# Six groups of source rows gathered from x without pacing, and GpSimd's wait for queries from group 12 on, in a two-layer graph network kernel

## The chip, the cores and the metric

The kernel runs on one core of one Trainium2 chip. The metric is the device time of one execution in microseconds. For the kernel before it is 2708.49 us, the median of three runs that lie between 2705.53 and 2711.26 us. The profile beside it is of one execution, whose span from the first to the last recorded instruction is 2246.1 us.

## The reference, cut to what matters

There are 3125 nodes with 128 features each and 103125 edges sorted by destination. The first layer is graph attention with four heads, followed by a small dense network; the second is a radial message passing layer over the same edges.

```python
# layer 1
q, k, v = x @ Wq.T + bq, x @ Wk.T + bk, x @ Wv.T + bv          # (3125, 4, 32)
alpha = sum(q[dst] * k[src], -1) / sqrt(32)
e = exp(alpha - segment_max(alpha, dst)[dst])
a = e / segment_sum(e, dst)[dst]
conv = segment_sum(a[:, :, None] * v[src], dst) + x @ Wskip.T + bskip
# ... Wout, layer norm, 128-512-128 MLP, layer norm; x = layernorm(x + that)
# layer 2
Y1 = sqrt(3) * edge_vec / (norm(edge_vec) + 1e-12)              # edge vectors
w = mlp(radial_embedding(edge_length)).reshape(-1, 4, 32)
messages = f(w, (x @ W_up)[src], Y1)                            # 256 numbers per edge
x = layernorm(x + segment_sum(messages, dst) @ W_out / 16)
```

## The kernel before, in words

Edges are handled in tiles of 128 and groups of four tiles (512 edges); there are 202 groups (`NQ`), and real edges fill 806 tiles (`REAL`). The kernel has four stages.

**Start.** SyncE loads the source numbers `src_col`, the weights `wqkv` and `bqkv` and the transposed x in four quarters (`xT`). ScalarE issues six loads of its own at once: `dst_rows`, `first_rows`, `consts`, `dst_i`, `base_i`, `r_col`. TensorE computes the queries of 26 node tiles (seven fours of tiles) and then keys and values of 25 (thirteen pairs); VectorE adds the bias (`q_sb` and `kv_sb` count its steps), SyncE writes the query table `q_tab` to DRAM, and ScalarE writes the key and value table `kv_tab`.

**Layer 1 over the edges.** For every group, GpSimd gathers four times 128 rows by source number, with one indirect DMA per tile. From group `XQ` on it gathers key and value rows from `kv_tab` (256 numbers per row) into a ring of 16 slots. For the first `XQ` groups the table isn't written yet, so it gathers rows of x itself (128 numbers) from an input in DRAM, and TensorE turns them (`x_turned`), ScalarE copies them (`x_copied`), TensorE multiplies them with the weights (`x_keys`), and VectorE adds the bias and puts the result into the slot (`x_biased`). The gathers of x have pacing waits: tiles 2, 4 and 6 wait for `q_sb`, tiles from 8 on for `kv_sb`. After them GpSimd waits for all of `kv_tab` and `q_tab`. The loop over groups on every engine is a list of slots. In slot q, TensorE makes the queries of group q+1 (`queries`, which counts `qe_ready`) from a window of `q_tab`; VectorE multiplies queries and keys (`product`), reduces them (`scores`), weighs values of the group 12 slots back (`weigh`, which counts `msg_ready`) and adds summed tiles to the accumulator (`add_tile`). Every eight groups a chain of small steps over four slots does the softmax of that batch. TensorE sums messages in `sums` (`sum_ready`). SyncE's queue loads, per group, `rel` (`numbers`) and four query windows (`windows`), ahead by up to six groups, and in between the rest: at group 3 the edge vectors `attr_col` and the writing of `r_far`, at group 5 a wait for `r_far`, from group 6 on the pieces of the radial embedding, at group 18 a wait for the finished edge directions (`yprep`) and the load of `x_rows`.

GpSimd's own waits in this stage are: from group 16 on for the ring slot (`msg_ready`), from group 6 on for the queries two groups back (`qe_ready` at q - 1), and before the third tile of a group for sums 15 groups back (`sum_ready`).

VectorE has, besides, one-time work on 128x808 arrays: the difference `rel_rows` ahead of the first query bias, the squares of edge vectors (`square_norms`) in slot 5 and the directions in slots 7 and 8 (`directions`).

**Dense part,** then **layer 2 over the edges**, again with one indirect DMA per tile, from `up_tab`, and then the output.

Of the kernel before, what the change touches and what calls it, by code (L numbers as in the profile page):

```python
# [14 lines left out]
P = 128  # L15
# [3 lines left out]
U32 = mybir.dt.uint32  # L19
ALU = mybir.AluOpType  # L20
# [16 lines left out]
RING = 16  # L37
# [4 lines left out]
CHAIN = 4  # L42
XQ = 4
LAG = BQ + CHAIN
# [10 lines left out]
REAL = -(-E // P)  # L55
HS = BT + 1
BIG = 1e38
assert NQ % 2 == 0 and H * BT == P and NT * P >= E and 4 * NT <= NW
# [85 lines left out]
def build(nc, a, out):  # L144
    with ExitStack() as ctx:
# [209 lines left out]
        def _(sp):  # L355
# [6 lines left out]

            sp.wait_ge(rel_ready, 1)
            sp.dma_start(rel_far.rearrange("(p n) -> p n", p=P), rel_rows).then_inc(rel_out, 16)
            for g, tiles in enumerate(fours):
                sp.wait_ge(q_sb, g + 1)
                sp.dma_start(q_tab[tiles[0] * P:(tiles[-1] + 1) * P, :].rearrange("(t p) f -> p t f", p=P),
                             q_stage[:, g, 0:len(tiles) * D].rearrange("p (t f) -> p t f", f=D)).then_inc(q_out, 16)
# [44 lines left out]
            for q in range(NQ):  # L413
# [6 lines left out]
                if q == 3:  # L420
                    batch_rows(0)
                    sp.dma_start(yvec[:], a["attr_col"]).then_inc(ld["attr"], 16)
                    sp.dma_start(b2f[0:1, 0, :], a["mlp_b2"]).then_inc(b2_in, 16)
                    sp.wait_ge(r_ready, 2)
                    sp.dma_start(r_far.rearrange("(p n) -> p n", p=P), r_col).then_inc(r_out, 16)
                if q == 5:
                    sp.wait_ge(r_out, 16)
                if emb_step(q, 6) is not None:
                    spread_lengths(emb_step(q, 6))
# [48 lines left out]
        def _(pool):  # L478
            pool.wait_ge(ld["src"], 16)
            for q in range(XQ):  # L480
                for k in range(QT):
                    t = q * QT + k
                    if k % 2 == 0 and 1 <= t // 2 <= 3:
                        pool.wait_ge(q_sb, t)
                    if k % 2 == 0 and t // 2 >= 4:
                        pool.wait_ge(kv_sb, 3 * (t // 2) - 11)
                    nc.gpsimd.indirect_dma_start(
                        xg[:, q, k, :], None, a["x_tab"],
                        bass.IndirectOffsetOnAxis(src_col[:, t:t + 1].bitcast(U32), 0)).then_inc(rows_in[q], 16)
            pool.wait_ge(kv_out, 16 * len(pairs))  # L490
            pool.wait_ge(q_out, 16 * len(fours))
            for q in range(XQ, NQ):
                if q >= RING:
                    pool.wait_ge(msg_ready, q - RING + 1)
                if q >= 6:
                    pool.wait_ge(qe_ready, q - 1)
                for k in real_tiles(q):
                    t = q * QT + k
                    summed = len([j for j in range(NQ) if weigh_slot(j) <= q - 3])
                    if k == 2 and summed:  # L500
                        pool.wait_ge(sum_ready, summed)
                    nc.gpsimd.indirect_dma_start(  # L502
                        kvr[:, q % RING, k, :], None, kv_tab,
                        bass.IndirectOffsetOnAxis(src_col[:, t:t + 1].bitcast(U32), 0)).then_inc(rows_in[q % RING], 16)

# [5 lines left out]
            for q in range(NQ):  # L511
# [4 lines left out]
                for k in real_tiles(q):  # L516
                    t = q * QT + k
                    if k == 2 and q >= 6:
                        pool.wait_ge(sum2_ready, QT * (q - 2))
                    nc.gpsimd.indirect_dma_start(  # L520
                        upr[:, q % RING, k, :], None, up_tab,
                        bass.IndirectOffsetOnAxis(src_col[:, t:t + 1].bitcast(U32), 0)).then_inc(rows_in[q % RING], 16)

# [271 lines left out]
        @block.scalar  # L795
        def _(act):
            act.dma_start(dst_rows, a["dst_rows"]).then_inc(ld["rows"], 16)
            act.dma_start(first_rows, a["first_rows"]).then_inc(ld["rows"], 16)
# [82 lines left out]
            for q in range(-3, LAST_SLOT):  # L881
# [11 lines left out]
                if q in SKIPS:  # L893
                    skipped(SKIPS.index(q))
                if q == 6:
                    act.wait_ge(yprep, 5)
# [118 lines left out]
        def _(dve):  # L1015
# [11 lines left out]
            v.memset(tile_sum[0:1].rearrange("p k (h t) -> p k h t", h=H)[:, :, :, 0], 0.0).then_inc(rows_ready, 1)  # L1027
            dve.wait_ge(ld["rows"], 32)
            v.tensor_tensor(rel_rows, dst_rows, first_rows, ALU.subtract).then_inc(rel_ready, 1)

            dve.wait_ge(ld["w"], 32)
            for g, tiles in enumerate(fours):
# [3 lines left out]
                                ps[:, 4 + g % 4, 0:n * D].rearrange("p (t f) -> p t f", t=n),  # L1036
                                bqkv[:, 0:D].unsqueeze(1).to_broadcast([P, n, D]), ALU.add).then_inc(q_sb, 1)
            for g, tiles in enumerate(pairs):
                n = len(tiles)
# [5 lines left out]
            def x_biased(g):  # L1045
                dve.wait_ge(xkv_mm, g + 1)
                for i in range(2):
                    v.tensor_tensor(kvr[:, g, 2 * i:2 * i + 2, :], ps[:, x_banks(g)[i], :].rearrange("p (t f) -> p t f", t=2),
# [187 lines left out]
            for q in range(LAST_SLOT):  # L1236
# [31 lines left out]
                if q == 4:  # L1268
                    bias_pieces()
                if q == 5:  # L1270
                    square_norms()
                if q in (7, 8):
                    directions(q - 7)
                if q == 34:
# [7 lines left out]
                if q == 11:  # L1282
                    dve.wait_ge(yprep, 12)
                    dve.wait_ge(r_out, 16)
                    dve.wait_ge(acc_zero, 1)


# [312 lines left out]
```

## Time and profile before

| | |
|---|---|
| runs, us | 2705.53 to 2711.26, median 2708.49 |
| profiled execution: span, us | 2246.1 (what lies around the span isn't recorded) |
| indirect DMAs of GpSimd | 16 from x, 790 from kv_tab, 806 from up_tab |
| GpSimd busy on the 790 from kv_tab, us | 762.0, first at 40.4, last at 1049.6 |
| GpSimd busy on the 806 from up_tab, us | 768.4, first at 1198.4 |
| PE, DVE, ACT, POOL busy, share of the span | 77%, 77%, 56%, 69% |

The trace gives each instruction its start and length, and the idle time of its engine before it with what ended it. "PE" is TensorE, "DVE" VectorE, "ACT" ScalarE, "POOL" GpSimd, "SPq" and "ACTq" the DMA issues of SyncE and ScalarE. GpSimd issues an indirect DMA for 0.94 to 0.95 us and takes 0.30 us before the next one; those 0.30 us are counted as idle, put down to "issue" or to a semaphore that was set before.

### The profile page before, as it was taken

What the parts mean: (1) busy time and instruction counts of PE and PEld (TensorE: products, weight loads), DVE (VectorE), ACT (ScalarE), POOL (GpSimd) and SP (SyncE); (2) the same over time, 40 slices, a digit from 0 to 9 for tenths busy, and PEclk for the clock granted to TensorE, in tenths of its full rate; (3) what the DMA queues carried; (4) which work ended last, traced back from release to release, by engine and by line L of the source; (5) the groups of instructions that cost most, each with busy time, mean ns of one, the idle gap of its engine ahead of it and who ended that gap; (6) DMA issues with size and microseconds to landing.
All of it is one profiled execution on the core that took longest, in us unless ns stands there. A gap on an engine that the chain in (4) does not pass through costs nothing. (4 is left out here: it accounts for less than half of the span.)

```text
span 2246.1 us, 37849 instructions
## 1 busy us (share of the span) xinstructions
PE 1725.3 (77%) x9754; PEld 1318.5 (59%) x9754; DVE 1727.8 (77%) x4978; ACT 1261.2 (56%) x3062; POOL 1552.3 (69%) x1617
## 2 busy tenths in 40 slices
PE   5657667676777767666588888888898889888886
PEld 5456556565666656555465565655565556556555
DVE  4778787776777777778686888888888888888887
ACT  1567667576675775766365455444444444545444
POOL 4777777777777777775015777777777777777773
PEclk9676776766666676776598999999999999999998
DMA  9787767677666676774001222222222222222221
GB/s 292 197 250 200 197 182 197 185 195 198 185 193 191 190 201 184 192 201 113 1 21 47 57 57 57 56 56 57 56 57 56 56 57 56 57 57 57 57 55 51
DMA packets 242692, 270.81 MB, mean 121 GB/s; under 512 B 46237, under 2 KB 201971, under 8 KB 241965
## 3 DMA queue, kind: packets, MB, share of 16 engines
q0 software_dynamic: 64224, 157.52, 25.8%
q1 hardware_dynamic: 173980, 105.40, 16.6%
q10 hardware_dynamic: 4272, 5.48, 0.7%
q8 instruction: 80, 1.31, 0.2%
q14 instruction: 136, 1.11, 0.2%
HBM read 256.06 MB, written 12.15 MB: 119 GB/s over the span
## 5 line engine op out<-in xcount | busy, mean ns | idle before, releaser
L520 POOL DMA_INDIRECT rows<-up_tab,src_col x806 | 768.4, 953 | 264.9 <-issue 239.9
L502 POOL DMA_INDIRECT rows<-kv_tab,src_col x790 | 762.0, 965 | 253.1 <-issue 218.2
L763 PE MATMUL ps<-hotT,rows 128*128 128x128 f32 x3232 | 426.0, 287 | 128.0 <-DVE rows L1452 128.0
L763 PEld LDWEIGHTS ps<-hotT,rows 128*128 128x128 f32 x3232 | 390.5, 197 | 201.7 <-DVE rows L1452 200.5
L1421 DVE TENSOR_TENSOR acc<-acc,ps 128x256 f32 x808 | 339.1, 420 | 95.6 <-DVE acc L1421 40.3
L582 PE MATMUL ps<-hots,msg 128*128 128x128 f32 x1616 | 337.8, 375 | 78.4 <-DVE msg L1135 72.1
L582 PEld LDWEIGHTS ps<-hots,msg 128*128 128x128 f32 x1616 | 295.0, 274 | 116.2 <-DVE msg L1135 110.3
L1116 DVE TENSOR_TENSOR work<-ps,rows 128x512 f32<-128x512 f32 x202 | 138.9, 688 | 205.5 <-issue 122.7
L571 PE MATMUL ps<-qwin,hotT 128*128 128x128 f32 x1088 | 217.5, 365 | 78.8 <-DVE work L1116 70.1
L816 ACT ACTIVATE hotT<-consts,nrel 128x128 f32<-128x128 f32 x808 | 255.5, 389 | 4.7 <-PE ps L763 4.7
L1152 DVE TENSOR_TENSOR acc<-acc,ps 128x128 f32 x808 | 227.4, 281 | 39.3 <-DVE acc L1152 4.2
L816 ACT ACTIVATE hots<-consts,nrel 128x128 f32<-128x128 f32 x808 | 255.5, 386 | 3.4 <-PE ps L582 3.2
L571 PEld LDWEIGHTS ps<-qwin,hotT 128*128 128x128 f32 x1088 | 197.5, 271 | 94.3 <-issue 75.2
L752 PE MATMUL ps<-weights,rows 128*128 128x256 f32 x808 | 231.2, 409 | 0.0
L978 ACT ACTIVATE rows<-ps,vecs 128x512 f32<-128x512 f32 x101 | 69.4, 687 | 265.9 <-PE ps L735 265.9
L984 ACT ACTIVATE rows<-ps,vecs 128x512 f32<-128x512 f32 x101 | 69.4, 687 | 237.4 <-PE ps L741 237.4
L752 PEld LDWEIGHTS ps<-weights,rows 128*128 128x128 f32 x808 | 138.5, 191 | 99.5 <-issue 88.7
L1436 DVE TENSOR_TENSOR rows<-rows,yvec 128x384 f32<-128x384 f32 x202 | 116.1, 575 | 96.8 <-DMA rows<-up_tab,src_col 95.8
L834 ACT ACTIVATE hotT<-rel,consts 128x512 f32<-128x512 bf16 x202 | 143.3, 709 | 7.0 <-DMA rel<-rel_far 5.5
L571 PE MATMUL ps<-exb,hotT 128*128 128x128 f32 x528 | 109.3, 375 | 43.6 <-DVE work L1116 37.7
L861 ACT COPY tile_max<-ps 1x256 f32<-1x256 f32 x26 | 9.4, 361 | 237.0 <-PE ps L611 237.0
L1126 DVE TENSOR_REDUCE alpha<-work 128x16 f32<-128x512 f32 x202 | 137.5, 681 | 0.8 <-issue 0.5
(178 smaller groups left out, 2496.6 us busy)
## 6 DMA issues: line engine op xcount, KB each, us to landing
qwin<-q_tab SPq DMA_DIRECT2D x544, 64.0 KB
rel<-rel_far SPq DMA_DIRECT2D x202, 128.0 KB
exb<-q_tab SPq DMA_DIRECT2D x264, 64.0 KB
rows<-up_tab,src_col POOLq DMA_INDIRECT x806
rows<-kv_tab,src_col POOLq DMA_INDIRECT x790
rows<-emb_rows SPq DMA_DIRECT2D x202, 16.0 KB
weights<-r_far SPq DMA_DIRECT2D x25, 128.0 KB, 3.7
emb_rows<-weights SPq DMA_DIRECT2D x25, 128.0 KB, 3.5
```

What stands on the lines that cost most here:

```text
L502: nc.gpsimd.indirect_dma_start(kvr[:, q % RING, k, :], None, kv_tab, bass.IndirectOffsetOnAxis(src_col[:, t:t + 1].bitcast(U32), 0)).then_ ...
L520: nc.gpsimd.indirect_dma_start(upr[:, q % RING, k, :], None, up_tab, bass.IndirectOffsetOnAxis(src_col[:, t:t + 1].bitcast(U32), 0)).then_ ...
L571: mm = pe.matmul(ps[:, 1 + q % 2, k * P:(k + 1) * P], hotT[:, q % TURNS, k, :], qrows(q)[:, k, :], start=True, stop=True)
L582: mm = pe.matmul(ps[:, 4 + j % SUMS, k * P:(k + 1) * P], msg0[:, j % 3, k, :], hot_of[:, j % HOTS, k, :], start=True, stop=True)
L752: mm = pe.matmul(to[:, k], h2s[:, u, (2 * half + k) * P:(2 * half + k + 1) * P], wt(W_M2, 2 * P).rearrange("p (s f) -> p s f", s=2), start ...
L763: mm = pe.matmul(ps[:, 4 + 2 * (q % 2) + k // 2, (2 * (k % 2) + m) * P:(2 * (k % 2) + m + 1) * P], left[:, q % 2, k, :], hot2[:, q % 2, k, ...
L816: op = nc.scalar.activation(to[:, k, :], iota, ACT.Square, bias=nrel[:, q * QT + k:q * QT + k + 1])
L834: nc.scalar.activation(to, rel[:, q % RELS, :], ACT.Square, bias=consts[:, K_NEGP:K_NEGP + 1]).then_inc(squareT_ready, 1)
L1116: v.tensor_tensor(work[:, q % 2, :].rearrange("p (t f) -> p t f", t=QT), ps[:, 1 + q % 2, :].rearrange("p (t f) -> p t f", t=QT), kvr[:, q ...
L1126: v.tensor_reduce(to, work[:, q % 2, :].rearrange("p (t h c) -> p t h c", t=QT, h=H), AX.X, ALU.add).then_inc(score_ready, 1)
L1152: v.tensor_tensor(to, to, ps[:, 4 + j % SUMS, k * P:(k + 1) * P], ALU.add).then_inc(acc_step, 1)
L1421: v.tensor_tensor(to, to, ps[:, 4 + 2 * (q % 2) + k // 2, (k % 2) * 256:(k % 2) * 256 + 256] .rearrange("p (m f) -> p m f", m=2), ALU.add) ...
```

## The change

- `XQ` goes from 4 to 6: six groups (24 indirect DMAs instead of 16) gather rows of x and go through TensorE. The pacing waits of these gathers are taken away. Two groups fewer (8 indirect DMAs) gather from `kv_tab`.
- GpSimd's wait for queries holds from group 12 (`FREE`) on, instead of 6.
- ScalarE's six loads are issued after the second quarter of `xT` has landed.
- `rel_rows` is computed after the fifth query bias instead of ahead of the first, and SyncE writes it after the fifth write to `q_tab`.
- The load of the edge vectors goes from group 3 to group 8, their squares from slot 5 to 11, ScalarE's root from 6 to 12, the directions from slots 7 and 8 to 13 and 14, and VectorE's wait for them from 11 to 16. SyncE's wait for them stays at group 18.
- `x_biased(4)` waits for the writes of `q_tab`, whose staging lies in the same bytes as slots 4 and up.
- The very last tile gathers only its real rows (85 of 128).

```diff
-XQ = 4
+XQ = 6
+FREE = 12
...
-            sp.wait_ge(rel_ready, 1)
-            sp.dma_start(rel_far.rearrange("(p n) -> p n", p=P), rel_rows).then_inc(rel_out, 16)
             for g, tiles in enumerate(fours):
+                if g == 5:
+                    sp.wait_ge(rel_ready, 1)
+                    sp.dma_start(rel_far.rearrange("(p n) -> p n", p=P), rel_rows).then_inc(rel_out, 16)
                 sp.wait_ge(q_sb, g + 1)
...
                 if q == 3:
                     batch_rows(0)
-                    sp.dma_start(yvec[:], a["attr_col"]).then_inc(ld["attr"], 16)
...
+                if q == 8:
+                    sp.dma_start(yvec[:], a["attr_col"]).then_inc(ld["attr"], 16)
...
             for q in range(XQ):
                 for k in range(QT):
                     t = q * QT + k
-                    if k % 2 == 0 and 1 <= t // 2 <= 3:
-                        pool.wait_ge(q_sb, t)
-                    if k % 2 == 0 and t // 2 >= 4:
-                        pool.wait_ge(kv_sb, 3 * (t // 2) - 11)
                     nc.gpsimd.indirect_dma_start(
...
-                if q >= 6:
+                if q >= FREE:
                     pool.wait_ge(qe_ready, q - 1)
...
         def _(act):
+            act.wait_ge(ld_x[1], 16)
             act.dma_start(dst_rows, a["dst_rows"]).then_inc(ld["rows"], 16)
...
-                if q == 6:
+                if q == 12:
                     act.wait_ge(yprep, 5)
                     nc.scalar.activation(ysq0, ysq0, ACT.Sqrt).then_inc(yprep, 1)
...
-            dve.wait_ge(ld["rows"], 32)
-            v.tensor_tensor(rel_rows, dst_rows, first_rows, ALU.subtract).then_inc(rel_ready, 1)
...
+                if g == 4:
+                    dve.wait_ge(ld["rows"], 32)
+                    v.tensor_tensor(rel_rows, dst_rows, first_rows, ALU.subtract).then_inc(rel_ready, 1)
...
             def x_biased(g):
                 dve.wait_ge(xkv_mm, g + 1)
+                if g == 4:
+                    dve.wait_ge(q_out, 16 * len(fours))
...
-                if q == 5:
+                if q == 11:
                     square_norms()
-                if q in (7, 8):
-                    directions(q - 7)
+                if q in (13, 14):
+                    directions(q - 13)
...
                 if q == 11:
-                    dve.wait_ge(yprep, 12)
...
+                if q == 16:
+                    dve.wait_ge(yprep, 12)
```

## Rows read from the trace of the kernel before

**Rows 1.** GpSimd's waits, 200 to 1000 us: line, releaser: us, times, longest us
```profile
POOL rows L502 <- issue: 174.9, 574, 0.3
```

**Rows 2.** GpSimd's waits, 0 to 1060 us
```profile
POOL acc L487 <- DVE rows L1035: 8.8, 1, 8.8
POOL rows L502 <- DMA kv_tab<-rows: 4.9, 1, 4.9
```

**Rows 3.** GpSimd's lines: count, busy us, mean ns, idle before
```profile
L502 POOL DMA_INDIRECT rows<-kv_tab,src_col x790 | 762.0, 965 | 253.1 <-issue 218.2 <-PE ps L571 22.4 <-PE ps L582 6.7
L520 POOL DMA_INDIRECT rows<-up_tab,src_col x806 | 768.4, 953 | 264.9 <-issue 239.9 <-DMA up_tab<-exb 19.5 <-PE ps L752 4.3
```

**Rows 4.** GpSimd in order of time: start, length, tile, idle before
```profile
6.29 1.08 POOL L487 DMA_INDIRECT acc<-in_x_tab,src_col  x1 [5.83 <-DMA src_col<-in_src_col]
40.42 0.95 POOL L502 DMA_INDIRECT rows<-kv_tab,src_col  x1 [4.89 <-DMA kv_tab<-rows]
58.40 0.94 POOL L502 DMA_INDIRECT rows<-kv_tab,src_col  x1 [8.03 <-PE ps L571]
63.41 2.33 POOL L502 DMA_INDIRECT rows<-kv_tab,src_col  x1 [0.30 <-issue]
102.39 0.95 POOL L502 DMA_INDIRECT rows<-kv_tab,src_col  x1 [0.30 <-issue]
```

**Rows 5.** Stages of the start: length; busy (count) of PE, PEld, DVE, ACT, POOL; PEclk, DMA share, GB/s
```profile
5.00:10.00 5.00, 0.00 (x0) 0.00 (x0) 1.00 (x1) 0.00 (x0) 2.57 (x2) 1.00 1.02 315
15.00:20.00 5.00, 5.00 (x36) 5.00 (x37) 2.78 (x5) 0.00 (x0) 1.71 (x2) 1.00 0.72 235
35.00:40.00 5.00, 3.60 (x14) 3.09 (x15) 0.94 (x2) 2.67 (x5) 0.53 (x1) 0.76 1.08 359
```

**Rows 6.** DMA issues: count, KB each, us from issue to landing
```profile
kv_tab<-rows ACTq DMA_DIRECT2D x12, 256.0 KB, 5.9
base_i<-in_dst_first ACTq DMA_DIRECT2D x1, 404.0 KB, 11.5
yvec<-in_attr_col SPq DMA_DIRECT2D x1, 1212.0 KB, 7.6
```

**Rows 7.** Issues of ScalarE and SyncE, and the first matmul, in order of time
```profile
12.68 2.05 PE L536 MATMUL ps<-wqkv,xT 128*128 128x128 f32 x8 [12.68 <-DMA xT<-in_xT]
26.96 1.27 SPq L376 DMA_DIRECT2D rel<-rel_far  x2
54.06 0.33 SPq L376 DMA_DIRECT2D rel<-rel_far  x1
69.92 1.90 SPq L387 DMA_DIRECT2D exb<-q_tab  x4
72.80 1.88 SPq L387 DMA_DIRECT2D exb<-q_tab  x4
109.78 0.42 SPq L434 DMA_DIRECT2D acc<-in_x_rows  x1
```

**Rows 8.** VectorE and TensorE from 67 to 103 us, in order of time
```profile
67.24 1.00 DVE L1070 TENSOR_TENSOR acc<-acc 128x808 f32<-128x808 f32 x1
79.81 0.68 DVE L1116 TENSOR_TENSOR work<-ps,rows 128x512 f32<-128x512 f32 x1
84.60 2.68 DVE L1080 RECIPROCAL acc<-acc 128x404 f32<-128x404 f32 x1
87.31 1.42 DVE L1082 SCALAR_TENSOR_TENSOR yvec<-yvec,acc 128x1212 f32<-128x1212 f32 x1
95.27 0.62 DVE L1116 TENSOR_TENSOR work<-ps,rows 128x512 f32<-128x512 f32 x1
99.06 1.92 PE L571 MATMUL ps<-qwin,hotT 128*128 128x128 f32 x8
```

**Rows 9.** VectorE's waits, 200 to 1000 us
```profile
DVE work L1116 <- issue: 111.8, 66, 3.4
DVE work L1116 <- DMA rows<-kv_tab,src_col: 39.0, 25, 2.5
```

More of the change, by code:

```diff
@@ L56 @@
 HS = BT + 1
+LAST_ROWS = E - (REAL - 1) * P
 BIG = 1e38
@@ L501, in _ @@
                         pool.wait_ge(sum_ready, summed)
+                    n = P if t < REAL - 1 else LAST_ROWS
                     nc.gpsimd.indirect_dma_start(
-                        kvr[:, q % RING, k, :], None, kv_tab,
-                        bass.IndirectOffsetOnAxis(src_col[:, t:t + 1].bitcast(U32), 0)).then_inc(rows_in[q % RING], 16)
+                        kvr[0:n, q % RING, k, :], None, kv_tab,
+                        bass.IndirectOffsetOnAxis(src_col[0:n, t:t + 1].bitcast(U32), 0)).then_inc(rows_in[q % RING], 16)
             pool.wait_ge(conv, NCH)
@@ L519, in _ @@
                         pool.wait_ge(sum2_ready, QT * (q - 2))
+                    n = P if t < REAL - 1 else LAST_ROWS
                     nc.gpsimd.indirect_dma_start(
-                        upr[:, q % RING, k, :], None, up_tab,
-                        bass.IndirectOffsetOnAxis(src_col[:, t:t + 1].bitcast(U32), 0)).then_inc(rows_in[q % RING], 16)
+                        upr[0:n, q % RING, k, :], None, up_tab,
+                        bass.IndirectOffsetOnAxis(src_col[0:n, t:t + 1].bitcast(U32), 0)).then_inc(rows_in[q % RING], 16)
         @block.tensor
```

## The prediction

> **What bounds the kernel now.** I read GpSimd's waits first, because its two lines of indirect DMAs fill two long stages. Between 200 and 1000 us it waits 174.9 us for "issue", 574 times, never over 0.3 [rows 1]. So 0.30 us is the gap between two gathers, and a gather costs 0.95 + 0.30 = 1.25 us, a group of four 5.0 us. 790 gathers (762.0 us busy, 253.1 idle before them) are the whole length of layer 1's edge stage [rows 3]. Over the whole start and stage there are only three real stalls: 8.8 us in the gathers of x (a pacing wait) and 4.9 us for `kv_tab` [rows 2], and 8.0 us for queries [rows 4]. In order of time: first gather of x at 6.29, the first from `kv_tab` at 40.42 after 4.89 idle, eight of them (groups 4 and 5), then 8.03 idle until the queries of group 4 are there, and group 6 at 58.40 [rows 4]. Up to the gather at 102.39, the first of group 14, it is 32 gathers in 44.0 us: 1.25 each, and 4 us for some that took longer beside VectorE, such as the one of 2.33 us at 63.41 [rows 4]. VectorE, on the other hand, waits at its product for 111.8 us ("issue") and 39.0 us (rows from `kv_tab`) in the same 800 us [rows 9]: in 20 batches of eight groups that is 7.5 us of slack in each 40 us. Layer 2 has the same form: 806 gathers, 768.4 us busy [rows 3]; the change touches it only in its last tile. So the kernel's end is the time of GpSimd's first gather for group 6, plus 782 gathers (tiles 24 to 805) at 1.25 us, plus a tail and a layer 2 that don't change. What counts is how early group 6 starts and how often GpSimd waits after it.
>
> **Part 1: groups 4 and 5 from x.** Eight gathers leave the `kv_tab` stream: 8 x 1.25 = 10.0 us from the path. They are added to the gathers of x: 24 x 1.25 = 30.0 us. From 6.29 us (perhaps one or two earlier, below) they end at 36.3, about 36.8 with the lengthened ones (the first is 1.08). `kv_tab` releases GpSimd at 40.4 [rows 4], so they hide in idle time: the pacing stall of 8.8 us and the 4.9 us for `kv_tab` [rows 2] are that idle time, 13.7 us against 10.0. If `kv_tab` came much earlier, 36.8 would be the floor: a further gain of 3.6 at most.
>
> **Part 2: no wait for queries before group 12.** The 8.03 us stall [rows 4] goes. With part 1 that is 58.40 - 40.42 = 18.0 us, if `kv_tab` stays where it is.
>
> **Part 3: when `kv_tab` is there.** For it: TensorE starts its first matmul at 12.68, when the first quarter of xT has landed [rows 7], while ScalarE's six loads (five of 404 KB, one of 130) take their share of DMA engines that are full (share 1.02, 315 GB/s) [rows 5]. Deferred, they leave 1.2 MB ahead of that quarter, which I estimate at 7 to 8 us; the last bias of keys comes up to 5 us earlier. Against it: the same bytes still have to move before 40 us, and the engines are full to the end (share 1.08, 359 GB/s, from 35 to 40) [rows 5]. The eight more gathers of 64 KB are 0.5 MB; at 0.33 MB per us that is 1.6 us; the one slack stretch (0.72 from 15 to 20 us) [rows 5] gives 1.4 us back. ScalarE's writes of `kv_tab` stand behind its own late loads in its queue. I take 0 for the sum of all that, with +4.6 us (50 GB/s less for the writes of 3.2 MB) and -3.6 (the floor) as ends. The trace shows no execution with the loads deferred, so the ends are kept for the range.
>
> The Trainium skill (DMA: Bandwidth & Descriptors, "Queues, rings and completion order") says that each DMA engine takes turns between the queues that have work, packet by packet. By that rule the unpaced gathers take from xT's loads and from `kv_tab`'s writes in their own turn, whatever was queued first, and it speaks against the removal of the pacing. No row of before separates the queues' shares in that stretch; by the rule the sum would be about 1.6 us smaller, and without it unchanged.
>
> **Part 4: SyncE's loads and the small moves.** `rel_rows` and its write now come later, `base_i` too (11.5 us to landing) [rows 6]. SyncE's first `rel` goes out at 26.96, when `q_tab` has landed [rows 7]. With issue at 10.5 + 11.5 us `base_i` is there at 22, and `rel_far` (issued at about 17, 10 us) at 27: no change, up to 3 us either way, and only queries hang on it. At group 5 SyncE now stands until 54.06 [rows 7] for `r_far`, which is queued behind the 1212 KB of edge vectors (7.6 us to land) [rows 6]; with these at group 8 it comes about 2 to 3 us earlier. Added work on TensorE, ScalarE and VectorE for two more groups of x lies in slots that wait for SyncE's windows: 0. The last tile: 0.
>
> **Part 5: the gates from group 12 on.** Group 6 at 40.4 puts group 12 at 70.4 and 14 at 80.4. At 12 GpSimd needs queries of group 10. Their windows went out at 69.92, those of group 11 at 72.80 [rows 7]; now I put group 10 at about 66, landing at 70 to 71 behind the edge vectors, queries at 72: a wait of 0 to 2. At 14 it needs queries of group 12. Before, they were made from 99.06 to 100.98 [rows 8] and used at 102.39 [rows 4]: 1.4 us of slack. Product 8 comes at about 64 instead of 79.81 (windows of group 8 and its rows are the later of its inputs); from it to product 10 it was 15.5 us [rows 8], of which 4.5 are directions (0.4 + 2.68 + 1.42, as in the rows of 84.60 and 87.31), which are gone from here: 11.0. Then 5.7 more to the end of queries 12: 64 + 11 + 5.7 = 81. A wait of about 1. The squares (five operations of 1.0 to 1.3 us, the last in [rows 8]; 5.8 us) and directions (2 x 4.5) then slow slots 11 to 14, and after that the chain of batch 1 starts: by the same counting sums 3 to 7 come within 2 us of where GpSimd wants them. The 4 us of lengthened gathers come again, later: 0. I take 2.0 us of waits, between 0 and 8 (8 being the old stall paid again).
>
> **Sum.** -10.0 - 8.0 + 0 + 2.0 = -16.0 us on the span: 2246.1 becomes 2230. The runs' median is 2708.49, which is 462 us more than the span; nothing recorded says whether that lies around the span or within. If around, it stays. If it were spread over the 1612 indirect DMAs, it would be 0.29 us on each; 24 gathers of x would then end at about 43.5, and group 6 would gain 58.4 - 43.5 = 15, with fewer waits at the gates. Both give the same answer to 1 us: 2708.5 - 16 = 2692.5 us.
>
> **Rivals.**
> (a) The gates take most of it back. If the windows of groups 9 to 12 land 6 us later (the edge vectors' load stands before them, and 1212 KB are 4 us of all engines), GpSimd waits at 12 and 14 for 8 to 14 us instead of 2. For it: 1.4 us of slack at group 14. Against: SyncE runs at 2.9 us per group there (69.92 to 72.80) [rows 7], against 5 for GpSimd. Gain 4 to 10: 2698 to 2704.
> (b) The start comes out better: `kv_tab` at 37, no waits at the gates, gain 21 to 22: 2687. For it: TensorE 5 us earlier. Against: full DMA engines.
> (c) `kv_tab` comes late, at 48 or more, since ScalarE's queue has 2.15 MB of loads ahead of the writes and three queues share the engines: gain 10 or less, 2698 to 2701. Against: bytes counted above.
> (d) Slower: SyncE stands at group 18 for the directions, which are now finished in slot 14 and not in slot 8. Before, they were done at 88.7 (87.31 + 1.42) [rows 8] and SyncE came to group 18 at 109.78 [rows 7]: 21 us to spare. Now directions end at about 104 (product 10 at 75; 7 to 8 us for slots 10 and 11; squares 5.8; three slots of 2.2, estimated from three VectorE operations of 0.68; directions 9.0), SyncE is there at about 90 and waits, and with it the windows of group 19, which lie behind a load of 1600 KB; from the directions' end to the queries of 19 it's about 9 us. GpSimd needs these for group 21, at 40.4 + 75 + 2 = 117. So it waits for directions that end after 108, and the kernel is slower than before if they end after 108 + 16 = 124. For that slots 8 to 14 would have to take 60 us instead of 40. Time then 2712 or so.
>
> **How the numbers follow.** The forecast (gain 10 to 20) has 0.70, (a) 0.12, (b) 0.06, (c) 0.07, (d) 0.05. A measurement of this kernel tells 0.2%, 5.4 us, from no change. Of (a) and (c) about 0.07 fall under that, the rest is faster: faster 0.87, same 0.08, slower 0.05. The range for 8 in 10 runs from 2687 (gain 21.5, the floor of part 1) to 2701 (gain 7.5, both late ends at once).
>
> **What would show it right or wrong.** In the changed kernel: 24 gathers of x at 1.25 us with no stall; the first gather from `kv_tab`, now group 6, at 40 +- 3 (part 3); none of GpSimd's waits over 0.3 until group 12, about 30 us later; waits there of 2 us in sum (part 5); the last gather from `kv_tab` at 1033 to 1034 instead of 1049.6; all later stages of the same length. A first matmul that isn't earlier than 12.68, a wait of GpSimd in every batch, or a stage 2 of another length would prove the account wrong.

## The result, and the profile after

The changed kernel takes 2732.04 us (median of 4 runs, 2728.52 to 2733.65) against 2709.88 us before (2705.53 to 2718.27) beside it on the same chip. The ratio is 1.0077, 95% interval [1.0061, 1.0093]. The forecast was 16 us faster; it is 22 us slower.

GpSimd's waits of the kernel after, over the whole span and then for 200 to 1000 us (line, releaser: us, times, longest):

```profile
...
POOL rows L503 <- issue: 195.2, 629, 0.9
POOL rows L503 <- remote: 165.9, 72, 3.2
...
POOL rows L503 <- PE ps L584: 98.5, 50, 3.2
POOL rows L503 <- PE ps L573: 69.4, 28, 31.8
```

```profile
POOL rows L503 <- issue: 124.6, 401, 0.9
POOL rows L503 <- remote: 113.8, 49, 3.2
POOL rows L503 <- PE ps L584: 63.1, 33, 3.2
POOL rows L503 <- PE ps L573: 23.2, 17, 1.9
```

The second fence answers to [rows 1], where "issue" at 0.30 us was nearly all there was. ("remote" is a semaphore that another engine set and of which the profile doesn't tell the instruction.) GpSimd's lines, which answer to [rows 3]:

```profile
L522 POOL DMA_INDIRECT rows<-up_tab,src_col x806 | 794.0, 985 | 433.8 <-issue 202.1 <-PE ps L765 158.8 <-PE ps L754 25.6
L503 POOL DMA_INDIRECT rows<-kv_tab,src_col x782 | 745.2, 953 | 553.8 <-issue 195.2 <-remote 165.9 <-PE ps L584 98.5
```

A gather still costs 0.95 us. What has grown is the idle time: 553.8 us in front of 782 gathers, where 790 had 253.1. Layer 2, which the change touches in one gather, has 433.8 instead of 264.9. So a good part of the difference from the profile shown of before can't be the change (e0 below settles how much). The start, in order of time (start, length, instruction, idle before), answers to [rows 4] and [rows 7]:

```profile
4.13 1.12 POOL L487 DMA_INDIRECT acc<-in_x_tab,src_col  x1 [3.67 <-DMA src_col<-in_src_col]
...
8.96 3.28 PE L538 MATMUL ps<-wqkv,xT 128*128 128x128 f32 x15 [8.96 <-DMA xT<-in_xT]
...
17.62 0.69 DVE L1035 TENSOR_TENSOR rows<-ps,bqkv 128x512 f32<-128x512 f32 x1 [2.89 <-remote]
...
27.48 0.69 DVE L1035 TENSOR_TENSOR rows<-ps,bqkv 128x512 f32<-128x512 f32 x1 [9.16 <-remote]
...
37.99 0.69 DVE L1035 TENSOR_TENSOR rows<-ps,bqkv 128x512 f32<-128x512 f32 x1 [9.82 <-remote]
...
41.15 11.70 ACTq L808 DMA_DIRECT2D kv_tab<-rows  x13
...
58.12 0.95 POOL L503 DMA_INDIRECT rows<-kv_tab,src_col  x1 [24.17 <-DMA kv_tab<-rows]
...
72.37 10.55 SPq L390 DMA_DIRECT2D exb<-q_tab  x4
...
119.56 0.94 POOL L503 DMA_INDIRECT rows<-kv_tab,src_col  x1 [31.78 <-PE ps L573]
```

Two stretches stand out: the gathers of x, in which VectorE's biases come 10 us apart, and groups 6 to 11 from 58 to 88 us, whose queries aren't made. Stretches of the same kernel (length; busy (count) of PE, PEld, DVE, ACT, POOL; PEclk, DMA share, GB/s), which answer to [rows 5]:

```profile
15.00:20.00 5.00, 2.58 (x15) 2.22 (x14) 0.69 (x1) 0.00 (x0) 3.78 (x5) 0.87 1.03 344
...
30.00:35.00 5.00, 1.17 (x2) 0.58 (x2) 0.00 (x0) 0.00 (x0) 3.04 (x4) 0.50 0.28 68
35.00:40.00 5.00, 1.17 (x2) 0.29 (x1) 2.01 (x3) 0.00 (x0) 0.00 (x0) 0.50 0.08 22
...
75.00:80.00 5.00, 0.00 (x0) 0.00 (x0) 0.00 (x0) 0.00 (x0) 3.78 (x5) 0.50 0.48 135
```

While GpSimd gathers without a break, the three other engines come nearly to a stand from 25 us on, and the DMA engines are far from full from 30 us on.

### The profile page after: what moved, and what is told of

The parts are those of the page before. It is cut to its first block and busy times, and to the rows that moved or that the text cites. A ratio compares the mean times of both kernels' runs of the same rounds, so it can differ in the third digit from the quotient of the medians.

```text
span 2731.9 us, 37909 instructions
## 1 busy us (share of the span) xinstructions
PE 1835.2 (67%) x9778; PEld 1411.8 (52%) x9778; DVE 1733.1 (63%) x4982; ACT 1252.8 (46%) x3064; POOL 1567.9 (57%) x1617
## 5 line engine op out<-in xcount | busy, mean ns | idle before, releaser
L503 POOL DMA_INDIRECT rows<-kv_tab,src_col x782 | 745.2, 953 | 553.8 <-issue 195.2
L522 POOL DMA_INDIRECT rows<-up_tab,src_col x806 | 794.0, 985 | 433.8 <-issue 202.1
L765 PE MATMUL ps<-hotT,rows 128*128 128x128 f32 x3232 | 509.0, 316 | 187.9 <-DVE rows L1458 109.7
L765 PEld LDWEIGHTS ps<-hotT,rows 128*128 128x128 f32 x3232 | 466.1, 224 | 261.5 <-DVE rows L1458 153.7
L987 ACT ACTIVATE rows<-ps,vecs 128x512 f32<-128x512 f32 x101 | 69.3, 686 | 631.3 <-remote 625.2
L612 PE MATMUL ps<-consts,fw 128*1 128x128 f32 x52 | 19.0, 366 | 347.0 <-DVE bw L1178 207.3
L754 PE MATMUL ps<-weights,rows 128*128 128x256 f32 x808 | 243.9, 427 | 0.0
L743 PE MATMUL ps<-rows,weights 128*128 128x512 f32 x202 | 127.9, 721 | 16.4 <-ACT rows L981 13.3
```

What stands on the lines that cost most here:

```text
L503: nc.gpsimd.indirect_dma_start(kvr[0:n, q % RING, k, :], None, kv_tab, bass.IndirectOffsetOnAxis(src_col[0:n, t:t + 1].bitcast(U32), 0)).t ...
L522: nc.gpsimd.indirect_dma_start(upr[0:n, q % RING, k, :], None, up_tab, bass.IndirectOffsetOnAxis(src_col[0:n, t:t + 1].bitcast(U32), 0)).t ...
L743: pe.matmul(ps[:, 1, :], wt(W_M1), h1s[:, n % 2, :], start=True, stop=True).then_inc(h2_mm, 1)
L754: mm = pe.matmul(to[:, k], h2s[:, u, (2 * half + k) * P:(2 * half + k + 1) * P], wt(W_M2, 2 * P).rearrange("p (s f) -> p s f", s=2), start ...
L765: mm = pe.matmul(ps[:, 4 + 2 * (q % 2) + k // 2, (2 * (k % 2) + m) * P:(2 * (k % 2) + m + 1) * P], left[:, q % 2, k, :], hot2[:, q % 2, k, ...
```

## Experiments

Ratios are to the kernel before timed beside it on the same chip, with 95% intervals. Before itself measured 2682.35 (e0 to e3), 2712.11 (e4 to e6), 2709.91 (e8 to e11), 2676.10 (e12 to e15) and 2710.34 us (e16 to e18; the same chip as e4 to e6), so times are compared within such a group.

### e0 to e3: which part costs

**e0**, the kernel before, unchanged.

> The kernel before, unchanged, profiled beside the others. Theory T (the trace that the prediction used is of a faster execution than the timed ones): its span comes out near its time, some 2705 us and not 2246, and GpSimd, which stood still only three times in the old trace, waits for other engines in both layers; the gap between group 6 of kv_tab's gathers and the span's start may be the old 58 us. Theory S (the changed kernel alone has stalls, made by its start): the span is near 2250 again and GpSimd's gathers stand 1.25 us apart as before, so that the stalls of 450 us seen after the change belong to the change.

Measured: 0.9983 [0.9966, 1.0000]. The profiled run took 2681.4 us for a span of 2679.6, so 1.8 us lie around the span. The 2246.1 us of the profile ahead of the prediction belong to a much faster execution than any timed one. Waits of e0 from 200 to 1000 us, and its lines:

```profile
POOL rows L502 <- issue: 130.5, 407, 2.4
POOL rows L502 <- remote: 84.6, 43, 3.0
POOL rows L502 <- PE ps L582: 54.6, 24, 3.2
POOL rows L502 <- PE ps L571: 46.0, 29, 2.7
```

```profile
L520 POOL DMA_INDIRECT rows<-up_tab,src_col x806 | 789.3, 979 | 422.0 <-issue 205.2 <-PE ps L763 134.3 <-PE ps L752 33.8
L502 POOL DMA_INDIRECT rows<-kv_tab,src_col x790 | 755.5, 956 | 501.5 <-issue 200.5 <-remote 130.0 <-PE ps L571 84.1
```

In the timed condition GpSimd waits 185.2 us of 800 for the other engines (84.6 + 54.6 + 46.0), in pieces of up to 3.2 us, where the old trace has nothing over the 0.3 us gap [rows 1]. The 433.5 us between the two spans: layer 1 from group 6 to the last gather takes 1230.6 us instead of 991.2 (+239.4), layer 2's gathers 1191.2 instead of 1012.4 (+178.8), all the rest +15.3.

**e1**, the change with its pacing waits put back.

```diff
                     t = q * QT + k
+                    if k % 2 == 0 and 1 <= t // 2 <= 3:
+                        pool.wait_ge(q_sb, t)
+                    if k % 2 == 0 and t // 2 >= 4:
+                        pool.wait_ge(kv_sb, min(13, 3 * (t // 2) - 11))
```

> The changed kernel with the pacing waits of the gathers of x put back (six groups; tiles 2, 4, 6 wait for query biases, tiles from 8 on for key biases). Theory A (the 24 unpaced gathers hold back VectorE's query biases, which came at 11, 14, 18, 27 and 38 us, and with them kv_tab, at 58 us): the biases are 0.9 us apart again, kv_tab is there at about 40 us, and the time falls by 18 to 25 us against the changed kernel, to 2707 to 2714. Theory B (ScalarE's deferred loads, or the order of rel_rows, hold VectorE back): no change, 2730.

**e2**, the change with ScalarE's loads issued at once.

```diff
-            act.wait_ge(ld_x[1], 16)
```

> The changed kernel with ScalarE's six loads issued at once, as before. Theory B (the deferred loads hold VectorE at rel_rows, in front of the sixth query bias, and base_i late): kv_tab is there at 45 us or earlier and the time falls by 12 to 20 us, to 2712 to 2720. Theory A (the unpaced gathers are what holds the start): kv_tab stays at 55 to 60 us and the time within 5 us of 2732.

**e3**, the kernel before with nothing but the later gate.

```diff
-                if q >= 6:
+                if q >= 12:
                     pool.wait_ge(qe_ready, q - 1)
```

> The kernel before with one edit: GpSimd's wait for queries holds from group 12 on. By my prediction's step for the stall of 8 us it gains 6 to 8 us (2701 to 2703). If in the timed executions GpSimd isn't the bound, because other engines are slower than in the old trace, it gains nothing (2708 +- 3), or loses some us by gathers that compete with the query windows.

Measured: e1 1.0045 [1.0025, 1.0065], e2 1.0070 [1.0048, 1.0092], e3 1.0070 [1.0044, 1.0096]. Putting the pacing back brings the first write of `kv_tab` from 41.15 to 18.23 us and the first gather from it to 44.89:

```profile
44.89 0.94 POOL L507 DMA_INDIRECT rows<-kv_tab,src_col  x1 [0.30 <-issue]
...
104.27 0.94 POOL L507 DMA_INDIRECT rows<-kv_tab,src_col  x1 [29.70 <-PE ps L577]
```

In e0, on the same chip, group 6 starts at 63.14 and group 12 at 97.9. So in e1 the start of group 6 is 18.2 us earlier, which is what parts 1 and 2 of the prediction promise, and the wait of 29.70 us at group 12 takes it all back: group 12 is 6.4 us later than in e0. Without ScalarE's wait (e2) the first gather from `kv_tab` comes at 59.7, as late as with it (58.1 in the change), and the loss is the change's. And e3, where one number differs from before, is 0.7% slower by itself. e3 in order of time:

```profile
72.50 14.17 SPq L387 DMA_DIRECT2D qwin<-q_tab  x4
...
83.75 0.69 DVE L1116 TENSOR_TENSOR work<-ps,rows 128x512 f32<-128x512 f32 x1 [26.17 <-remote]
83.77 0.95 POOL L502 DMA_INDIRECT rows<-kv_tab,src_col  x1 [0.30 <-issue]
83.81 0.72 ACT L834 ACTIVATE hotT<-rel,consts 128x512 f32<-128x512 bf16 x1 [17.92 <-remote]
...
84.58 1.83 PE L571 MATMUL ps<-exb,hotT 128*128 128x128 f32 x7 [16.83 <-issue]
...
116.84 0.94 POOL L502 DMA_INDIRECT rows<-kv_tab,src_col  x1 [32.13 <-PE ps L571]
```

From 44.99 to 84.71 GpSimd issues 32 gathers, 1.25 us apart. VectorE stands for 26.17 us in them, ScalarE for 17.92, TensorE for 16.83, and four window loads of SyncE take 14.17 us where they took 1.88 [rows 7]. All four move again within 1 us of the last gather's start. Then GpSimd stands for 32.13 us: group 6 starts 8.2 us earlier than in e0 (54.97), as part 2 says, and group 12 18.9 us later (116.84), so the gate at group 12 gives back all that the missing gate at 6 had saved, and more. It isn't one trace alone. In the change, e1, e2, e4 and e18, VectorE stands for 16 to 24 us in the row of gathers ahead of group 12, and moves again 1.6 to 5.8 us after that row's last gather has started.

### e4 to e6: both parts, one after the other

**e4** is the change again, **e5** the change with `FREE = 6`, **e6** the change with `FREE = 6` and the pacing of e1.

> The changed kernel again, on one chip with the next three, so that the parts can be added up (the other chip gave 1.0077 of the kernel before). My theory now (D): a train of back-to-back indirect DMAs on GpSimd makes the semaphore increments of the other engines arrive late, so that what lengthens a train (no pacing in the gathers of x, no wait before group 12) costs time; it expects 1.006 to 1.009 here too, with group 12 of kv_tab's gathers at 115 to 120 us against 98 before. Rival (R): the loss on the other chip lies in that chip's conditions; then this is within 0.3% of before.

> The changed kernel with GpSimd's wait for queries from group 6 on again (one number, 12 to 6); everything else of the change stays, the unpaced gathers of x too. Theory D: the 24 gathers for groups 6 to 11 no longer form one train, so the stall of 30 us before group 12 goes, and 8 to 15 us of the loss with it: 1.001 to 1.004 of before. Rival R2 (it is the start, up to kv_tab's landing at 58 us, that costs everything): unchanged, 1.007.

> As the last one, and with the pacing waits of the gathers of x put back: of the change there remain six groups from x, the deferred loads of ScalarE and of the edge vectors, and rel_rows' new place. Theory D: both long trains are gone, kv_tab is there at about 44 us, and the eight gathers taken off the kv_tab stream gain at last: 0.994 to 0.999 of before. R2 or a theory in which the extra x groups cost other engines more: 1.000 to 1.003.

Start of GpSimd's gathers in us, from the traces:

| | ratio | group 6 | group 12 | group 20 | last from kv_tab |
|---|---|---|---|---|---|
| e4 | 1.0066 [1.0042, 1.0090] | 58.1 | 115.1 | 167.4 | 1328.2 |
| e5 | 1.0042 [1.0027, 1.0056] | 69.9 | 104.7 | 156.8 | 1317.6 |
| e6 | 0.9997 [0.9984, 1.0011] | 60.6 | 95.8 | 148.1 | 1308.7 |

The later gate costs 10.4 us by group 12 and 10.6 by the last gather (e4 against e5), the missing pacing 8.9 and 8.9 (e5 against e6). The loss arises ahead of group 12 and stays as it is. In the times it is 7.8 and 12.8 us (2729.14, 2721.31, 2708.47). With both undone, the change is level with before: what is left of it, six groups from x among it, is worth nothing. In e6 GpSimd is through with its 24 gathers of x and then stands 17.55 us for the queries of group 4:

```profile
12.64 0.95 POOL L491 DMA_INDIRECT acc<-in_x_tab,src_col  x1 [6.17 <-DVE rows L1039]
...
60.63 0.94 POOL L507 DMA_INDIRECT rows<-kv_tab,src_col  x1 [17.55 <-PE ps L577]
```

### e8 to e11: is it the break between gathers?

**e8**, the kernel before with four memsets of 128x32 behind each group of layer 1, each with a wait for the one before. They write bytes that nobody reads.

```diff
+                    for _ in range(4 if k == 3 else 0):
+                        if rests:
+                            pool.wait_ge(rested, rests)
+                        nc.gpsimd.memset(rest[:], 0.0).then_inc(rested, 1)
+                        rests += 1
```

**e9** has one such memset behind every gather. **e10** is e6 with the gate at the queries of the group before (`qe_ready` at q instead of q - 1). **e11** does the same in layer 2 too (`w_mm` at q).

> The kernel before, with four short memsets on GpSimd (128x32 each, with GpSimd's own semaphore between them, an estimated 0.15 to 0.3 us each) after each group of four gathers of layer 1. If GpSimd alone were the bound (the prediction's account), 198 groups times 0.6 to 1.2 us come on top: 1.04 to 1.09 of before. Theory D (trains of back-to-back indirect DMAs delay the others' semaphore increments): GpSimd's waits, now 260 to 290 us in this stage, take up the memsets, the trains get shorter, and the period of a group stays at 6.3 to 6.4 or falls: 0.97 to 1.01.

> The same work, spread: one such memset after each gather, so that no two gathers of layer 1 follow each other at 1.25 us. Theory D, if only unbroken trains at 1.25 us count: a larger gain than with the four together, 0.95 to 0.98. D, if the mean rate of indirect DMAs counts: the same time as with the four together, within 0.3%. GpSimd as the only bound: 1.04 to 1.09.

> The kernel of e6 (six groups from x, paced; wait for queries from group 6) with the wait one group tighter: gathers of group q wait for the queries of group q - 1 instead of q - 2. Theory D: the trains (mean 4.9 gathers, up to 13) get shorter, increments come in time more often, and the period falls below 6.40: 0.97 to 0.995. Rival L (GpSimd's lead is what hides the landing of the rows): VectorE's product waits for rows more often, 1.00 to 1.03.

> As e10, and in layer 2 too: gathers of group q wait for the edge weights (w_mm) of group q - 1 instead of q - 2. Theory D: layer 2, now 5.95 us per group with trains of 7.7 gathers in the mean, gains in the same way; another 0.5 to 2% over e10. Rival L: layer 2 gets longer by the landing of rows, up to 1% slower than e10.

Measured: e8 0.9753 [0.9728, 0.9778], e9 1.0011 [0.9998, 1.0024], e10 1.0012 [0.9990, 1.0034], e11 1.0133 [1.0095, 1.0172]. First e9 and then e8, GpSimd in order of time:

```profile
200.12 0.95 POOL L504 DMA_INDIRECT rows<-kv_tab,src_col  x1 [0.17 <-issue]
201.08 0.14 POOL L510 MEMSET rest<- 128x32 f32 x1
201.38 0.95 POOL L504 DMA_INDIRECT rows<-kv_tab,src_col  x1 [0.17 <-issue]
```

```profile
205.83 0.95 POOL L504 DMA_INDIRECT rows<-kv_tab,src_col  x1 [0.30 <-issue]
206.78 0.68 POOL L510 MEMSET rest<- 128x32 f32 x4
208.04 0.95 POOL L504 DMA_INDIRECT rows<-kv_tab,src_col  x1 [0.58 <-issue]
```

Both kernels run four memsets per group. In e9 each hides in the 0.30 us between two gathers, which stay 1.26 us apart, so GpSimd's pace is as before and nothing changes. In e8 they make one break of 1.26 us (0.84 in most groups below 16), and the kernel is 2.5% faster although GpSimd has more to do: 101.4 us of memsets. e8 from 200 to 1000 us, and its line:

```profile
POOL rows L504 <- issue: 193.5, 508, 0.9
POOL rows L504 <- remote: 7.4, 11, 1.2
POOL rows L504 <- DVE msg L1142: 4.0, 6, 1.2
POOL rows L504 <- PE ps L589: 2.2, 2, 1.3
```

```profile
L504 POOL DMA_INDIRECT rows<-kv_tab,src_col x790 | 758.9, 961 | 317.2 <-issue 285.1 <-remote 12.4 <-DMA kv_tab<-rows 6.7
```

The waits for other engines are 13.6 us, and a group takes 6.08 us (from 200 us to the end of the stage). In e9, on the same chip, they are 183.5 us and 6.42; in e0, on another, 185.2 and 6.30. A break also slows GpSimd: with it a group can't take less than 6.0 us (three times 1.25, 0.95 and 1.26), without it 5.0. Pauses of the same sum spread evenly over the gathers weren't tried, so whether the break as such helps or the slower pace isn't shown. What the other engines do while GpSimd gathers, counted from the traces of layer 1 by the place of a gather in its row of gathers without a break of over 0.4 us:

```
instructions per us of PE, PEld, DVE and ACT, while the gather at this place runs
place            1-4     5-8     9-12
e0              12.5     8.3     0.5
after           13.2     8.2     0.4
e8              10.1      -       -
e10             11.4     6.5     9.5
```

This counting can't tell cause from effect by itself, since a row also ends where the others have stopped and GpSimd's gate holds it. e10 speaks against taking the length of a row for the whole cause. From 200 us on its rows are 6.9 gathers long in the mean, against 4.9 in e6 (another chip), the period is the same (6.40 and 6.41 us per group), and at places 9 to 12 the others work on; its breaks are fewer and longer, 269.7 us in sum against 280.7. In e11 layer 2 takes 6.12 us per group where e10 takes 5.94 (from 1600 us on), with waits of 205.0 us for "remote" before its gathers: a tighter gate there costs. Of these four expectations of the theory of rows only e8's held: e9 and e10 were to gain and did not, and e11 went with the rival.

### e12 to e15: the change with breaks

**e12** is the change with the four memsets behind each group of x and of layer 1, **e13** the kernel before with them in both layers, **e14** e6 with them in x and both layers, **e15** the kernel before with two per group in layer 1.

> The changed kernel whole, with the four short memsets after each group of gathers of x and of kv_tab (a pause of 1.26 us instead of 0.30, as seen in e8). In e8 the kernel before with the same pauses in layer 1 was 0.9753 of before. Theory D (the change costs time because its trains of 24 gathers hold up the other engines): with trains cut to four the change's cost of 0.7 to 0.8% is gone, and its eight gathers fewer gain: 0.966 to 0.976. Rival E (the change costs by something else, such as the deferred loads or two more groups of x on TensorE and VectorE): the cost stays, 0.981 to 0.985.

> The kernel before with the pause of four memsets after each group of gathers in both layers. Theory D: layer 2, at 5.94 us per group with trains of 7 to 8 gathers, gains too, up to the new floor of 5.95 us of GpSimd's own work per group: since that floor is where it already stands, little, -0.5 to +0.5% over e8, 0.970 to 0.980. If the pauses add to layer 2 instead: 0.98 to 1.01.

> The kernel of e6 (of the change: six groups from x, paced; deferred loads; wait from group 6 on) with the pauses in the gathers of x and in both layers. e6 was 0.9997 of before. Theory D: as e13, less the 8 gathers (10 to 12 us at 1.49 per gather): 0.966 to 0.976. Rival E: as e13 or slower.

> The kernel before with two memsets instead of four after each group of kv_tab's gathers: a pause of some 0.7 to 0.8 us instead of 1.26 (e8) or 0.30 (before). Theory D, if any break of a train over about 0.3 us helps: period 5.5 to 5.7 us, 0.955 to 0.97. If only the mean rate of GpSimd's indirect DMAs counts, half of e8's gain or less: 0.985 to 1.0.

Measured: e12 0.9805 [0.9774, 0.9837], e13 0.9841 [0.9809, 0.9873], e14 0.9865 [0.9832, 0.9897], e15 0.9896 [0.9852, 0.9941]. Two memsets give 1.0% (a group takes 6.18 us; with four, in e13 on the same chip, 6.04), four in layer 1 alone 2.5% on other chips. In layer 2 the breaks lose: 6.03 us per group in e13, 5.89 in e12 (from 1600 us on). e12 and e14 missed the 0.966 to 0.976 that the theory of rows expected of them. e15 missed its 0.955 to 0.97 and lies where it was expected if only GpSimd's mean rate counts (0.985 to 1.0), so the slower pace stays a rival of the break.

### e16 to e18: the change against before, both with breaks, on one chip

**e16** is e8 again, **e17** e12 again, **e18** the change. As in e8 and against the words of its expectation, e16 has no breaks in the gathers of x; e17 has them there too.

> The kernel before with four small memsets on GpSimd (128x32, own semaphore) after each group of x and kv gathers of layer 1. Theory (trains of gathers hold back what the other engines report): about 0.975 of the kernel before again. Rival (the gain was of one chip alone): within 0.5% of before.

> The change with the same rests in the same places. Theory that the change's own loss is made by the longer trains alone: with the trains cut, the change is level with the rested kernel before (within 0.2% of it, on the same chip), or up to 0.6% faster, what the prediction gave it. Rival (the late gate costs by itself, by a wait for the queries of group 12 that no rest takes away): 0.3 to 0.7% slower than the rested kernel before.

> The change as it is, on the same chip as the two rested kernels, so that its loss without rests stands beside its loss or gain with them: 1.006 to 1.009 of before by every theory.

Measured: e16 0.9741 [0.9721, 0.9761] (2634.09 to 2643.35 us), e17 0.9781 [0.9758, 0.9805] (2645.59 to 2659.89), e18 1.0068 [1.0052, 1.0085]. The medians, 2636.46 and 2647.57, are 11.1 us or 0.42% apart, and the two sets of runs don't overlap. So breaks don't cure the change's own loss: they leave 11 of its 18 us, and the rival written down for e17 holds. What they do cure is the start. With the same unpaced gathers of x, `kv_tab`'s first write goes out at 41.09 in e18 and at 21.62 in e17, and the first gather from it starts at 59.03 and 44.17. GpSimd at both ends of the ungated stretch of e17:

```profile
44.17 0.96 POOL L514 DMA_INDIRECT rows<-kv_tab,src_col  x1 [6.00 <-DMA kv_tab<-rows]
...
75.69 0.95 POOL L514 DMA_INDIRECT rows<-kv_tab,src_col  x1 [0.30 <-issue]
76.64 0.69 POOL L490 MEMSET rest<- 128x32 f32 x4
100.15 0.95 POOL L514 DMA_INDIRECT rows<-kv_tab,src_col  x1 [22.82 <-PE ps L585]
```

Stretches of e16 and then of e17, with the columns as above:

```profile
60.00:70.00 10.00, 6.12 (x32) 3.73 (x30) 9.66 (x17) 7.24 (x12) 7.71 (x11) 1.00 0.62 180
70.00:80.00 10.00, 4.73 (x19) 2.97 (x19) 7.95 (x9) 4.20 (x6) 8.01 (x15) 0.82 0.68 191
```

```profile
60.00:70.00 10.00, 5.02 (x15) 4.20 (x16) 1.88 (x3) 1.83 (x3) 7.67 (x15) 0.50 0.51 144
70.00:80.00 10.00, 1.51 (x9) 1.23 (x8) 2.05 (x4) 1.27 (x3) 5.78 (x13) 0.67 0.38 104
```

In 20 us VectorE does 3.9 us of work in e17 and 17.6 in e16. Of the 17.6, 9.6 are the squares and directions, which the change does later, so like for like it is 3.9 against 8.0, beside a GpSimd that is busy for 13.5 and 15.7 us (in e17 it stops at 77.3). The length of the breaks isn't what differs: in both it is 0.84 us there (0.69 of memsets and 0.15). What does was not tried.

## Why the prediction was wrong

**What bounds the kernel: the step that failed.** The prediction read one execution of 2246.1 us in which GpSimd never waits [rows 1], and concluded that the end is a start plus 782 gathers at 1.25 us. e0 shows that this doesn't hold in the timed condition: there a group takes 6.30 us and not 5.0, GpSimd waits for the others, and e8 is faster with more work on GpSimd. An earlier gather is only worth something if the others can follow. e1 shows the step most plainly: group 6 starts 18.2 us earlier than in e0, where 18.0 were forecast, and group 12 6.4 us later. In e3, where the later gate is the only edit, the long row of gathers goes with a standstill of the others that ends with the row.

**The sum's treatment of the 462 us.** It said that nothing tells whether they lie around the span or within, and that "both give the same answer". Within was right (1.8 us lie around), and the answer was not the same. The prediction spread them as 0.29 us on each indirect DMA, which left GpSimd as the bound; in fact a gather kept its 1.25 us and the time went into waits for the other engines. The doubt was seen and priced with the wrong mechanism. A span 17% under the timed runs should have taken most of the weight off every argument that rests on slack of a microsecond.

**Part 1 (-10.0).** That 24 gathers of x take 30 us was right (4.13 to 33.95). That they hide was wrong: without pacing or breaks, they hold back the biases from which `kv_tab` is made (e18 against e17), and GpSimd then waits 24.17 us for it. With pacing they do hide (e1), but in e6 they bring nothing, because the queries of group 4 are what comes next: 17.55 us.

**Part 2 (-8.0).** The old stall goes, as said. What comes in its place is four times as long: a wait of 31.78 us at group 12 for the queries that weren't made while GpSimd ran on. e3 shows it alone (32.13 us).

**Part 3 (0, ends +4.6 and -3.6).** The first matmul comes earlier, at 8.96 instead of 12.68, as forecast. The table comes at 58.12 instead of 40 +- 3, 13 us beyond the later end kept for it (40.4 + 4.6). It was priced as bytes on DMA engines that are full. (The +4.6 doesn't follow from the rates beside it either: 3.2 MB take 1.4 us longer at 309 GB/s than at 359.) They are full up to 20 us (share 1.03), but at 30 to 40 us, where the table is late, their share is 0.28 and 0.08. The Trainium skill (DMA: Bandwidth & Descriptors, "Queues, rings and completion order") says that a DMA engine takes turns between queues packet by packet. It pointed to the right edit, the lost pacing, and to the right sign; with 1.6 us it names too small a cause, since the loss lies where the engines had little to move.

**Part 4 (0).** ScalarE's wait is worth nothing that these runs can tell: e2 without it is 1.0070 and the change 1.0077, 1.0066 and 1.0068, with intervals that overlap. The moved one-time work wasn't tried by itself; e6, which keeps all of it and is level with before, bounds its sum with that of the two more groups of x.

**Part 5 (+2.0, ends 0 and 8).** This is the term of the sum that was furthest off: the gate costs 31.78 us of waiting where 2 were forecast. The working took VectorE's and SyncE's pace from an execution in which GpSimd's gathers did not touch it: windows every 2.9 us. Here one set of windows takes 10.55 us to issue.

**The rivals.** (a), the gates take it back, is the right place with too small a price (8 to 14 us). (c), `kv_tab` late at 48 or more, came true as well, at 58, by another cause. (d), the only slower one, did not happen: its late directions are not what GpSimd waits for at group 12. None held that GpSimd itself could be what the other engines wait for.

## What to carry to other kernels

Before any sum, compare the span of the profile with the timed runs, and where they differ by more than a little, take a profile that matches them: slack read from the faster one is worth nothing. A wait that only paces GpSimd can be what lets the others work, so before taking out a "useless" wait ask what runs during it. Where one core issues hundreds of indirect DMAs with other engines waiting on each other, try a short break per group, stage by stage; in layer 1 it gave 2.5% here, more than the 0.8% that the change was forecast to give at its best (21.5 us), and in layer 2 it cost.

## What the runs showed of the hardware that was not expected

- Rows of indirect DMAs on GpSimd without a break go with a near standstill of the rest. With 32 of them (e3, 40 us) the other engines started 0 instructions from 70 to 80 us; SyncE's four DMA issues took 14.17 us instead of 1.88.
- The standstill goes with semaphores that are recorded late. Of the increments by TensorE, VectorE and ScalarE, this share is recorded within 0.1 us of the end of the instruction that makes them. The columns go by where in a row of gathers the instruction ends; "between rows" is every break of over 0.4 us and all other times without gathers:

```
                      all    between rows   1st-2nd  5th-6th  9th-10th in a row
before, 2246.1 us    0.99        1.00         1.00     1.00     1.00
e0                   0.45        0.76         0.52     0.30     0.18
after                0.46        0.77         0.54     0.30     0.19
e8                   0.39        0.57         0.41     0.37     0.38
(rows of e8 beyond the 4th gather are of layer 2)
```

- They are late for a while after a row, too. In e0 the share is 0.20 in the first 0.5 us after the end of a row's last gather, 0.37 from 0.5 to 1 us, 0.84 from 1 to 2 us, and 0.99 or more later.
- e8 is faster without a higher share on time, so the breaks don't make the increments prompt. What holds the increments back stays open, and so does why the execution of 2246.1 us had none of it with 782 gathers in a row: a long row alone isn't enough for a standstill. Every timed execution here, of every kernel, has a recorded span 1.8 us under its time; whether the recording takes part in the delay can't be told from these runs. DMA bandwidth is an unlikely cause: the share is 0.45 to 0.46 in the standstill of e3.
- A break of 1.26 us behind each fourth gather of layer 1 gave 2.5%, in layer 2 it cost. Four single memsets that hide in the gaps between gathers, and so add no pause, gave nothing.
- TensorE's granted clock is 0.50 in the standstills, the lower of its two levels (1.2 GHz), with no matmul in the same stretch (75 to 80 us of the kernel after).
